# A larger share of the planned TensorE gaps is filled with transposes of the identity: FILL from .5 to .85 in a one-core decoder layer kernel

## What is computed

```python
x = x + attn(layernorm(x), w_qkv, w_o)        # 16 heads of 32, rotary, causal softmax
x = x + ssm(ctx, layernorm(x), in_proj_w, conv_w, conv_b, x_proj_w,
            dt_proj_w, dt_proj_b, A_log, D)
# ssm: u = silu(causal conv of 4 taps(in_proj(ctx)));  dt, B, C = x_proj(u)
#      delta = softplus(dt_proj(dt));  16 states: state = state*exp(delta*A) + delta*u*B
#      y = (sum over states of state*C + D*u) * silu(z),  z = layernorm(x)
x = x + ffn(layernorm(x), w_fc, w_proj)
# ffn: bitlinear -> gelu -> bitlinear; bitlinear normalises its input and multiplies
#      by weights rounded to -1, 0, +1 times their mean magnitude
```

## Time and profile before

| | |
|---|---|
| time, median of 3 runs | 970.25 us (968.16 to 970.95) |
| the profiled execution, its time | 970.87 us |
| the profiled execution, its span from first to last instruction | 969.1 us |
| TensorE's mean granted clock in it | 0.979 |
| busy share of the span: PE, DVE, ACT, POOL | 92%, 88%, 76%, 64% |
| idle-time transposes (L1708) | 190 |

### The profile page before, as it was taken

The page is one execution under the profiler, slowest core; times in us unless marked ns, Lnnn a source line. Parts: engine busy times, 40 slices in busy tenths (PEclk is TensorE's granted clock), DMA queues, the critical chain, the costliest instruction groups (busy, mean ns, idle before and its releaser), DMA issues.

```text
span 969.1 us, 17249 instructions
## 1 busy us (share of the span) xinstructions
PE 893.0 (92%) x5426; PEld 573.7 (59%) x5426; DVE 854.3 (88%) x1167; ACT 735.0 (76%) x1476; POOL 615.8 (64%) x439
## 2 busy tenths in 40 slices
PE   7998779889999999989999999789889999999998
PEld 5464546556776656677656577567745455544544
DVE  4698999999999979899998989999989989998741
ACT  4988955935757996786988775896589999999551
POOL 0286954655347638993663989535679889878620
PEclk9999999799999999999999999799999999999999
DMA  6678849778847555274734645643147566755383
GB/s 211 234 225 267 224 124 230 197 206 216 225 144 205 165 182 148 72 210 112 185 101 136 206 132 183 220 110 111 38 72 179 112 135 129 151 106 125 62 166 77
DMA packets 146296, 153.55 MB, mean 158 GB/s; under 512 B 90448, under 2 KB 94800, under 8 KB 145952
## 3 DMA queue, kind: packets, MB, share of 16 engines
q1 hardware_dynamic: 146208, 152.45, 59.0%
HBM read 103.00 MB, written 28.44 MB: 136 GB/s over the span
## 4 chain that ended last, share of the span: by engine, by line
PE 45%; ACT 17%; DVE 15%; issue 11%; POOL 8%; DMA 3%; SPq 1%; ACTq 0%; POOLq 0%; DVEq 0%
PE ps L1765 7%; PE ps L1891 7%; PE ps L1834 6%; PE ps L1881 5%; DVE hb L1911 5%; ACT p_q L1615 4%; POOL hb L1382 4%; PE ps L1808 3%; ACT ps L1502 3%; PE ps L1778 3%; PE ps L1846 3%; DVE y_acc L1933 2%; ACT p_t L1631 2%; PE ps L1739 2%; DVE m_col L2008 2%
## 5 line engine op out<-in xcount | busy, mean ns | idle before, releaser
L1382 POOL TENSOR_TENSOR hb<-du,b_bc 128x1024 f32<-128x1024 f32 (+1 forms) x160 | 308.4, 1951 | 93.1 <-PE ps L1834 87.3
L1911 DVE TENSOR_TENSOR_SCAN hb<-ps,hb 128x1024 f32<-128x1024 f32 (+1 forms) x128 | 256.6, 2012 | 15.8 <-ACT ps L1502 12.2
L1502 ACT ACTIVATE ps<-delta,a_neg 128x511 f32<-128x511 f32 (+2 forms) x320 | 179.4, 598 | 86.2 <-DVE hb L1911 82.0
L1933 DVE SCALAR_TENSOR_TENSOR y_acc<-ps,ct,y_acc 128x512 f32<-128x512 f32 x256 | 178.6, 736 | 14.0 <-PE ps L1834 13.3
L1834 PE MATMUL ps<-ident,hb 128*128 128x128 f32 x1088 | 150.7, 281 | 24.8 <-DVE hb L1911 8.3
L1834 PEld LDWEIGHTS ps<-ident,hb 128*128 128x128 f32 x1088 | 124.0, 143 | 55.4 <-issue 16.5
L1615 ACT ACTIVATE p_q<-ps,m_col 128x512 f32<-128x512 f32 (+3 forms) x256 | 132.0, 538 | 10.5 <-DVE m_col L2008 9.5
L1765 PE MATMUL ps<-xn_t,w_ring 128*128 128x512 f32 x256 | 120.7, 616 | 1.0 <-ACT p_t L1631 0.5
L1881 PE MATMUL ps<-t_fc,xt 128*128 128x512 f16 x512 | 116.6, 379 | 1.8 <-ACT h_sb L1679 1.8
L1891 PE MATMUL ps<-t_pr,ht 128*128 128x512 f16 x512 | 113.0, 379 | 0.5 <-DMA ht<-hs 0.5
L1631 ACT ACTIVATE p_t<-ps 128x512 f32<-128x512 f32 x160 | 86.0, 612 | 26.8 <-PE ps L1808 26.6
(11 more groups left out here) (137 smaller groups left out, 1484.2 us busy)
## 6 DMA issues: line engine op xcount, KB each, us to landing
w_ring<-in_w_attn SPq DMA_DIRECT2D x32, 512.0 KB, 4.5
qk_d<-hl SPq DMA_DIRECT2D x64, 256.0 KB
q_st<-qk_d SPq DMA_DIRECT2D x64, 256.0 KB, 4.4
b_bc<-bc_d SPq DMA_DIRECT2D x48, 256.0 KB, 4.5
raw<-in_w_fc SPq DMA_DIRECT2D x16, 512.0 KB, 4.6
raw<-in_w_pr SPq DMA_DIRECT2D x16, 512.0 KB, 5.2
k_st<-qk_d SPq DMA_DIRECT2D x32, 256.0 KB, 4.6
k_st<-qk_d SPq DMA_DIRECT2D x64, 128.0 KB, 4.7
```

Source lines behind the costliest of these rows:

```text
L1382: nc.gpsimd.tensor_tensor(piece_of(e, hi, lo).rearrange("p (a n) -> p a n", a=2), du[b % 2][:, 2 * h:2 * h + 2, lo:hi], b_bc[:, i % BC_RIN ...
L1502: ins = nc.scalar.activation(factors(j, hi, lo)[:, (hi - lo) * m + start:(hi - lo) * (m + 1)], delta[b % 2][:, et, lo + start:hi], ACT.Exp ...
L1911: v.tensor_tensor_scan(h, d, h, 0.0, ALU.mult, ALU.add).then_inc(scan_done, 1)
L1933: v.scalar_tensor_tensor(out=y, in0=bank(kind, r, tb), scalar=ct[:, b % 2, tb, n:n + 1], in1=y, op0=ALU.mult, op1=ALU.add).then_inc(y_free ...
```

## The change

One constant: the share of each foreseen gap that is filled goes from one half to 0.85.

```diff
 ISSUE, ISSUES = 0.46, {"xt": 1.3, "ht_ffn": 2.0, "stack": 3.4, "lo": 2.7}
-FILL, FILL_US = .5, 0.11
+FILL, FILL_US = .85, 0.11
```

## The result

| | before | after |
|---|---|---|
| median of 15 runs each | 969.11 us (966.44 to 975.1) | 973.62 us (969.93 to 975.56) |
| ratio, 95% interval | | 1.0039 (1.0023 to 1.0055), +3.8 us (2.2 to 5.3) |
| the profiled execution: time, span | 970.87, 969.1 us | 973.71, 971.9 us |
| mean granted clock in it | 0.979 | 0.984 |

The kernel is slower by 0.39% (0.23 to 0.55). The forecast was +6.1 us and 976.4 us, with a range of 971.3 to 980.5. The measured median lies in the range; the forecast's +6.1 us lies above the interval of the difference. In the following, an effect in us is the ratio's excess over 1 times 970 us, with its 95% interval; the two medians alone lie 4.5 us apart, inside that interval. The runs of these two kernels spread over some 6 to 9 us, so a single profiled execution can be some us off its median.

The account below looks back on a forecast made before the run. No engine bounds the run alone; the chain passes between engines, with idle-time transposes on it. Start 3.27, later chain places 4.25, off-chain 0.30, clock -1.70 sum to +6.1 us on 970.25: 976.4 us, range 971.3 to 980.5.

Parts of the forecast that it names:

- The start: ln1b(0,0), ln1b(0,1), inproj(0,0): data already there, so 30 added transposes at 0.109 us make everything start 3.27 us later.
- the covered places: Nine places with TensorE idle behind the transposes, such as xproj(0), xproj(1), ht(48,0), ht(52,0): added transposes cost 0 us.
- the end: proj(15), the last group of matmuls: 12 added transposes with nothing left to hide behind, counted in full, 1.31 us.
- sign of being wrong: The prediction is wrong if the start isn't later by about 3 us; first inproj matmul foretold at about 16.8, not 13.6.
- the clock, -1.70 us: Half-clock stretch at 79.4, over the matmuls of xproj(1): expected not to happen, 3.63 instead of 5.33 us, a 1.70 us gain.
- The step that looked for cover: At proj(15): data land at 958.5, when the sixteen transposes of before are through, so nothing hides the added ones.
- The late places of the middle: Chain places rot, s(30,0), wo(3,0,0), summing with the end to 4.25 us; late items off the chain, 0.3 us, bounds 0 to 2.4.
- every further transpose delays the item by its full length: Where transposes lie on the chain, the item's data are there first, so each added one costs 0.109 us at full clock.
- B: Rival: denser work also removes three half-clock stretches besides the one at 79.4, up to 1.7 us each: +1.0 us, 971.3 us; chance 0.18.
- the prediction's own sign for B: The mean granted clock rises above some 0.985, which would be several half-clock stretches gone.
- C: Rival: all late items off the chain count, 2.4 us, and the clock gives nothing back: +9.9 us, 980.2 us; chance 0.15.
- D: Rival: transposes hold no clock, so no gain at xproj(1), everything else as forecast: +7.8 us, 978.1 us; chance 0.05.

Follow-up runs that it names:

- the two runs that enclose it: Against the kernel before: larger numbers everywhere but the start, 970.81 us, ratio 1.0010; larger numbers at the nine covered places alone, 967.88 us, ratio 0.9977.
- Ten more in each of the six: Kernel before with ten more transposes at rot(0,2,0), rot(1,2,0), rot(1,2,1), rot(3,3,0), s(30,0) and wo(3,0,0): 974.69 us, ratio 1.0054.

## Why the prediction was right, and where it was not

**Direction, range and mechanism: right; the size is too large.** The kernel is slower because transposes were added ahead of items whose data were already there. The start with +2.2 us and the covered places with -2.2 us show both halves of the argument, and the end, made larger, costs its length. Of the forecast's +6.1 us, 3.8 (2.2 to 5.3) came.

**The start, 3.27 us: right.** 2.2 us (0.7 to 3.9) in time, 3.24 us as the difference of the means of seven and two traces. The first matmul of `inproj` came at 15.5 and not at the foretold 16.8, 2.1 us later than in the profile of before, since the clock rose late in the one profile (11.2) and early in the other (9.1). Taken by the letter, that was the prediction's sign of being wrong, "if the start isn't later by about 3 us"; it was a poor sign, since a single pair of profiles can't tell it.

**The end, 1.31 us: right,** 1.2 us in the traces and 4.26 us for forty. The step that looked for cover was too narrow, though: I took the last landing of one execution, which was slow, for the rule. In other executions the data are there before even the sixteen transposes are through.

**The covered places, 0 us, and the clock, -1.70 us: right in size,** -2.2 us (-3.8 to -0.8), **and by luck.** The prediction had one fall gone, the one at 79.4, for its full 1.70 us. It is gone in the trace, but ten more at `xproj(1)` alone gave -0.6 us (-2.7 to 1.6) and no less time at the half clock. What the runs show in its place is 7.4 us less at the half clock in the mean with all nine covered places larger, worth some 0.27 us each. Which of `xproj(0)`, `v(2,1,0)`, `ht(52,0)` and the others bring it isn't settled: no run took them one by one.

**The late places of the middle, 2.94 us on the chain and 0.3 off it: too much, and the step that failed.** The sum of these and the end was 4.55 us, and the two runs that enclose it give 3.2 us; less the 1.3 of the end, about 1.9 us is left, against 3.2. The intervals of these runs are too wide to prove it, but the traces show it place by place: 1.6 and 1.3 us lasted of 2.94, nothing at `rot(0,2,0)` and `s(30,0)`, and half at `wo(3,0,0)`. The 0.3 us off the chain is about right. The step was "every further transpose delays the item by its full length", taken over from the item to the end of the run: each item was delayed by its full length, and the next wait of TensorE took up some of it. A piece of the chain is a place where nothing was spare on the path that was followed back; where a long "issue" comes next, the path was a guess. Ten more in each of the six cost 5.2 of 6.5 us, so the small numbers of the change fell in part into slack that larger ones use up.

**The rivals.** B, the clock pays for it, is in part what happened. In the profiled pair about three stretches fewer stand at the half clock (0.979 to 0.984, just short of the prediction's own sign for B), and in the mean of the runs 5.2 us less. B's price of up to 1.7 us for each is what failed: the 1.4 us gained at 120.4 were lost in the next wait, and the result stayed slower. C, the covers fail, had 9.9 us, outside the interval, and the run of the covered places alone shows that their covers hold. D, transposes hold no clock, is excluded: in the kernel after nothing but transposes runs from 5.34 to 12.0, and 45 of them take 6.95 us, where the pace of the half clock in the earlier trace rows would need 9.5; and with no transposes anywhere the mean clock falls to 0.968. The rule of the Trainium skill, "TensorE: Matmul & The Clock Gate", Part 4 (PE-mode transpose), that transposes don't count as busy work for the clock, is not what these rows show for transposes of this kind.

## What to carry to other kernels

A filler on an in-order engine is free only where the trace shows idle time behind it that ends with the item's data; so place it and size it by the trace, and not by what a planner foresees. Here 68 more of the same instruction were worth -2.2 us in nine places, while at the start and the end each cost its full 0.109 us and in the middle anything from nothing to that; keeping it in the nine alone gave -6.3 us. And read a chain of waits as an upper bound: time added to it costs at most its length, and often less where the next wait has room or an "issue" piece follows; time taken away gained less still. A gain of the clock has to be checked in the mean clock of many runs, since a fall that one profile shows prevented may stand elsewhere.

## What the runs showed of the hardware

- The moment at which the clock rises at the start differs between executions of nearly the same program: with the same transposes, which began between 4.5 and 5.8 us, the clock rose between 8.5 and 11.6 us and the matmuls of `inproj` began between 11.5 and 13.6 us. That alone moves a single profile by 2 us.
- A gap of 2.06 us without a matmul ahead of `xproj(1)` was followed by the half clock in five of six profiled executions and not in the sixth. A single profile can't tell that a gap is harmless.
- Over 226 runs 0.27 us of execution time went with each us that TensorE spent at the half clock. That is about half of the 0.5 us that it would cost if TensorE bounded the run all along.
